# Last stage of an audio tower on one Trainium2 core: query/key/value at the end of the period in front, the norm ahead of them a period earlier, and another order of the experts' layers

## The reference, cut to what matters

```
h = tok(x)                                   # patches, matmul, norm: (32, 92, 128)
h = h + ssm(layernorm(h))                    # 16 states, a scan over time
h = h + moe(layernorm(h))                    # 6 experts, one chosen for each token
h = h + attn(layernorm(h))                   # window of 7 positions, 16 heads of 8
    q, k, v = x @ qkv_w.T + qkv_b
    p = softmax(q . k[window] * SCALE + rpb[...])      # 7 scores for each head
    attn = (sum over the 7 offsets of p * v[window]) @ proj_w.T + proj_b
h = h + ffn(layernorm(h))                    # 6 experts for each sequence
    ew = weights of 6 experts, from the mean over the sequence's tokens (router)
    ffn = sum over e of ew[e] * (gelu(x @ W1[e] + b1[e]) @ W2[e] + b2[e])   # 128 -> 341 -> 128
```

## Time and profile before

| | |
|---|---|
| median of 3 executions | 825.05 us (824.59 to 826.01) |
| the profiled execution | 826.72 us |
| its span, first to last instruction | 824.9 us |
| mean granted TensorE clock | 0.871 |
| busy: PE, PEld, DVE, ACT, POOL | 626.6, 475.1, 623.7, 518.4, 278.5 us |
| last stage, from about 542.6 us on | 282.3 us |

### The profile page before, as it was taken

One profiled execution on the slowest core, in us unless ns is written; L12 is line 12 of the kernel. 1 busy time (PEld: TensorE's weight loads), 2 busy tenths in 40 slices (PEclk: granted clock), 3 DMA queues, 4 the chain that ended last, 5 costly groups with the idle time before them and its releaser, 6 DMA issues.

```text
span 824.9 us, 10874 instructions
## 1 busy us (share of the span) xinstructions
PE 626.6 (76%) x3090; PEld 475.1 (58%) x3091; DVE 623.7 (76%) x1289; ACT 518.4 (63%) x821; POOL 278.5 (34%) x312
## 2 busy tenths in 40 slices
PE   6996751835637183659788799987899999999998
PEld 4563651835627173555565689844566666666665
DVE  1787598999999999999886122167698898896853
ACT  1587899899899998993243034352466466465452
POOL 0464000000000100000388244316357667664642
PEclk9997876958678695869767799999899999999999
DMA  5381042355444455540611366320000000000000
GB/s 181 112 292 49 1 86 41 73 99 107 73 86 86 73 102 98 92 86 0 224 33 39 102 175 191 90 65 1 1 0 7 4 11 8 2 10 7 5 10 18
DMA packets 26383, 56.50 MB, mean 68 GB/s; under 512 B 4203, under 2 KB 15572, under 8 KB 25860
## 3 DMA queue, kind: packets, MB, share of 16 engines
q0 software_dynamic: 5728, 24.56, 15.8%
q1 hardware_dynamic: 19848, 30.80, 12.2%
q10 hardware_dynamic: 764, 0.62, 0.2%
HBM read 29.91 MB, written 10.17 MB: 49 GB/s over the span
## 4 chain that ended last, share of the span: by engine, by line
PE 37%; DVE 27%; issue 15%; ACT 10%; POOL 5%; DMA 2%; POOLq 1%; SPq 1%; ACTq 0%; DVEq 0%
PE psum L2101 6%; PE psum L1797 4%; DVE s_R L1286 4%; DVE s_R L1273 4%; PE psum L2088 3%; POOL x_sorted L688 3%; PE psum L2016 3%; PE psum L2024 3%; DVE s_R L1297 3%; PE psum L1883 2%; PE psum L1884 2%; PE psum L1885 2%; PE psum L2090 2%; PE psum L2089 2%; PE psum L2191 2%
## 5 line engine op out<-in xcount | busy, mean ns | idle before, releaser
L1883 PE MATMUL psum<-s_xn_lo,s_split_hi 128*128 128x368 f32 x256 | 95.3, 372 | 134.9 <-ACT s_R L914 132.6
L1883 PEld LDWEIGHTS psum<-s_xn_lo,s_split_hi 128*128 128x128 f32 x256 | 55.0, 215 | 139.2 <-ACT s_R L914 135.3
L673 POOL DMA_DIRECT2D s_xnfm<-s_R x14 | 17.1, 1219 | 258.7 <-DVE s_R L1297 258.7
L1292 DVE TENSOR_TENSOR_SCAN s_R<-s_R 128x2944 f32<-128x2944 f32 x15 | 94.4, 6292 | 0.7
L1054 ACT ACTIVATE s_R<-psum,s_cols 128x368 f32<-128x368 f32 x96 | 50.3, 566 | 68.2 <-PE psum L2090 68.1
L1884 PE MATMUL psum<-s_xn_hi,s_split_lo 128*128 128x368 f32 x256 | 92.3, 361 | 0.0
L1885 PE MATMUL psum<-s_xn_hi,s_split_hi 128*128 128x368 f32 x256 | 91.9, 359 | 0.0
L2101 PE MATMUL psum<-s_R 128*128 128x368 f32 x256 | 90.5, 484 | 0.0
L732 POOL TENSOR_TENSOR s_R<-s_R 128x368 f32<-128x368 f32 x47 | 54.0, 1148 | 38.5 <-DVE s_R L1586 19.2
L769 POOL TENSOR_TENSOR s_R<-s_R 128x368 f32<-128x368 f32 x48 | 46.6, 970 | 57.7 <-DVE s_R L1722 56.9
L921 ACT ACTIVATE s_R<-psum,s_cols 128x736 f32<-128x736 f32 x64 | 56.1, 876 | 14.5 <-PE psum L1885 10.8
(11 more groups left out here) (260 smaller groups left out, 1617.0 us busy)
## 6 DMA issues: line engine op xcount, KB each, us to landing
s_xnfm<-s_R POOLq DMA_DIRECT2D x14, 1472.0 KB, 10.5
s_R<-in_w SPq DMA_DIRECT2D x28, 256.0 KB, 2.9
s_R<-in_xg SPq DMA_DIRECT2D x7, 744.0 KB, 4.2
x_sorted<-in_x_init SPq DMA_DIRECT2D x1, 5082.0 KB
s_wBC<-in_wBC SPq DMA_DIRECT2D x8, 256.0 KB, 2.6
s_R<-in_v SPq DMA_DIRECT2D x2, 1024.0 KB
s_R<-x_sorted SPq DMA_DIRECT2D x28, 66.0 KB, 2.4
s_R<-in_w SPq DMA_DIRECT2D x1, 1536.0 KB, 6.4
```

What stands on the lines that cost most here:

```text
L1292: dve.tensor_tensor_scan(bufB[:, u], ra[:, u], bufB[:, u], 0.0, ALU.mult, ALU.add).then_inc(ra_free, 1)
L1883: pe.matmul(bank(c), w_hi[:, s, u, k, :], xn_lo[:, a:b], start=True, stop=False)
```

## The change

Only the last stage is touched.

- PE: `qkv_of(c + 1)` stands at the end of period c, ahead of the last two tiles, `qkv_of(0)` ahead of the loop. The transposes of `norm_transposes(nE, c + 1)` stand in the middle of period c, ahead of `shares_fm`; their input is made a period earlier. `project` comes first in the period, then one tile, `scores`, one tile, `scores_tm`, and 8 tiles in a row. `fill_pause` is gone. `spread_out` names its two offsets.
- The list `FFN`: the rests' first layer comes as tiles 6 to 9, their second layer as 18 to 21; experts 3 and 4 have their first layer as 14 to 17; expert 5 is last with both layers. A chunk's units (6 experts and the rests) have their places in `UNITS`, and what counts units goes by `unit(f, e)`.
- DVE: `residual_stats` is split into `residual` and `stream_stats`, `first_experts` into itself and `experts_stats`. A period begins with the statistics of `experts_stats(c + 1)` left over from the one before, the experts' weights and `weigh_rest`, then the products; `scores_out` comes between `residual` and `stream_stats`. The 7 experts' units are weighed at other places. `first_experts(c + 2)` stands between offsets 1 and 2.
- ACT: `qkv_out(c + 1)` stands at the end of the period, `normed_e(c + 1)` at the start of the next; four gelus stand behind `stream_hi`, not ahead.
- POOL: `rstd_e(c + 2)` stands last in the period; `projection_bias`, `rstd_f` and the adds follow. `weighted_sum` is cut in four.

```diff
+        FFN = (pair(1, 0, 1, 2) + rest_of(1) + pair(2, 0, 1)
+               + pair(1, 3, 4) + rest_of(2) + pair(2, 2, 3, 4) + pair(1, 5) + pair(2, 5))
+        UNITS = (0, 1, NE, 2, 3, 4, 5)
...
             for c in range(NCH + 2):            # POOL
-                add_expert(c - 3, NE)
+                att = c < NCH
                 if 1 <= c <= NCH:
                     projection_bias(c - 1)
-                if c + 1 < NCH:
-                    rstd_e(c + 1)
-                add_expert(c - 2, 1)
+                    rstd_f(c - 1)
+                add_unit(c - 2, 1)
...
+                    weighted_sum(c, 3, 4)
+                if c <= NCH:
+                    add_unit(c - 2, 6)
+                if att:
+                    weighted_sum(c, 5, 6)
+                if c + 2 < NCH:
+                    rstd_e(c + 2)
...
+                if 1 <= c < NCH - 1:            # ACT
+                    normed_e(c + 1)
                 gelus(c - 2, 14, 16)
-                gelus(c - 2, 16, 18)
                 if c < NCH:
                     exponential(c)
-                gelus(c - 2, 22, 24)
+                    load_table(ACT.Gelu, 1)
+                rest_out(c - 2)
...
                     stream_hi(c - 1)
+                gelus(c - 2, 16, 18)
+                gelus(c - 2, 28, 30)
+                gelus(c - 1, 0, 10)
...
                     expert_weights(f - 1)       # DVE
-                weigh_expert(f - 1, 0)
-                weigh_expert(f - 1, 1)
...
+                weigh_rest(f - 1)
                 if att:
                     score_products(c)
...
-                store_chunk(c - 3)
                 if tail:
-                    residual_stats(f)
+                    residual(f)
                 if att:
                     scores_out(c)
+                if tail:
+                    stream_stats(f)
+                weigh_expert(f - 1, 0)
...
                 if att:                         # PE
                     scores(c)
-                ffn(f - 1, 18, 20)
+                ffn(f - 1, 15, 16)
                 if att:
                     scores_tm(c)
-                ffn(f - 1, 20, 22)
+                ffn(f - 1, 16, 24)
...
-                    if c >= 2:
-                        fill_pause(1)
                     shares_fm(c)
...
+                    spread_out(c, 0, 1)
...
+                ffn(f - 1, 26, 30)
+                ffn(f, 0, 1)
+                if tail:
+                    router_logits(f)
+                ffn(f, 1, 2)
+                if att:
+                    spread_out(c, 2, 3)
...
+                ffn(f, 6, 12)
+                if tail:
+                    router_spread(f)
                 if c + 1 < NCH:
-                    pe.wait_ge(pb_free, c * K + K - 1)
-                    norm_transposes(pe, nE, c % 2, c + 1, (7, 7))
+                    qkv_of(c + 1)
                 ffn(f, 12, 14)
```

More of the change, by code:

```diff
@@ L499, in audio_tower, with pair, rest_of @@
         out_done = [sem("out_done0"), sem("out_done1")]
-        FFN = ([(1, e, j) for e in (0, 1, 2) for j in range(FT)]
-               + [(2, e, j) for e in (0, 1) for j in range(FT)]
-               + [(1, 3, 0), (1, 3, 1)] + [(1, NE, r) for r in range(NR)]
-               + [(1, 4, 0), (1, 4, 1)] + [(2, e, j) for e in (2, 3) for j in range(FT)]
-               + [(1, 5, 0), (1, 5, 1)] + [(2, e, j) for e in (4, 5) for j in range(FT)]
-               + [(2, NE, r) for r in range(NR)])
+        def pair(layer, *es):
+            return [(layer, e, j) for e in es for j in range(FT)]
+        def rest_of(layer):
+            return [(layer, NE, r) for r in range(NR)]
+        FFN = (pair(1, 0, 1, 2) + rest_of(1) + pair(2, 0, 1)
+               + pair(1, 3, 4) + rest_of(2) + pair(2, 2, 3, 4) + pair(1, 5) + pair(2, 5))
+        UNITS = (0, 1, NE, 2, 3, 4, 5)
         ORDER1 = [(e, j) for layer, e, j in FFN if layer == 1]
@@ L762, in second_share, with weighted_sum @@
                 pool.tensor_tensor(zs[:, 1:2], euler, zs[:, 3:4], ALU.pow).then_inc(rt_exp, 1)
-            def weighted_sum(c, after_second):
-                for o in range(1, K):
+            def weighted_sum(c, *offsets):
+                for o in offsets:
                     pool.wait_ge(pb_free, c * K + o + 1)
@@ L1060, in rest_out @@
                     return
-                g = f * NU + NE
+                g = unit(f, NE)
                 act.wait_ge(fo_mm, g + 1)
@@ L1580, in weigh_expert @@
                     return
-                g = f * NU + e
+                g = unit(f, e)
                 if g >= 2:
@@ L1626, in score_products, with residual @@
                         .then_inc(prod_r, 1)
-            def residual_stats(c):
+            def residual(c):
                 dve.wait_ge(proj_mm, c + 1)
@@ L1730, in _ @@
                     expert_weights(f - 1)
-                weigh_expert(f - 1, 0)
-                weigh_expert(f - 1, 1)
-                if 0 <= f - 1 and not att:
-                    weigh_rest(f - 1)
-                if c + 1 < NCH:
-                    first_experts(c + 1)
+                weigh_rest(f - 1)
                 if att:
@@ L2172, in shares_fm, with spread_out @@
                 ins.then_inc(PT_ready, 1)
-            def spread_out(c, o):
-                if o % 2:
-                    return
+            def spread_out(c, o, *more):
+                two = (o,) + more
                 if o == 0:
@@ L2180, in spread_out @@
                     pe.wait_ge(P_fm_ready, c + 1)
+                    if 1 <= c < NCH - 1:
+                        pe.wait_ge(nE.xT_free, 2 + c + 2)
                     if c:
@@ L2185, in spread_out @@
                 else:
-                    pe.wait_ge(pb_free, c * K + min(o + 1, K - 1) - 2)
-                two = range(o, min(o + 2, K))
+                    pe.wait_ge(pb_free, c * K + two[-1] - 2)
                 for P, last in ((P_lo, False), (P_hi, True)):
@@ L2267, in _ @@
-                    norm_transposes(pe, nE, c % 2, c + 1, (7, 7))
+                    qkv_of(c + 1)
                 ffn(f, 12, 14)
-                if tail and not att:
-                    router_spread(f)
             result_last()
```

197 lines of the change are left out of this document (96 added, 101 removed).

## The result

| | before | changed |
|---|---|---|
| median of the runs, us | 825.14 (824.59 to 826.01, 4 runs) | 835.61 (835.31 to 836.22, 4 runs) |
| ratio changed / before | | 1.0119, 95% interval 1.0096 to 1.0143 |
| the profiled execution: time, span, us | 826.72, 824.9 | 836.22, 834.4 |

Forecast were 824.6 us, with a chance of 0.43 for slower, 0.41 for faster.

The account below looks back on a forecast made before the run. PE nearly binds, but DVE's chain through PE and POOL may decide. Middle periods -1.3, periods 0 and 1 -0.5, period 7 +0.4, tail +1.0: -0.4 us from 825.05, 824.6; range 816 to 836, likeliest case 820.5 to 829.

Parts of the forecast that it names:

- Rival (b): Middle periods: POOL stays shut out until the products end, residual at 10.1, period 32.75 us, total 834.9; chance 0.30.
- I am wrong if DVE has no idle time before the residual and yet the period is over 31: Middle period: the prediction's own condition for being wrong; the alternative condition was period 1's clock deciding the difference.
- case (a): Middle periods: POOL gets in between products, its bias holds DVE about 1.1 us, residual at 8.05, period 30.7; chance 0.45.
- an idle residual: Sign in the changed profile: residual with idle time ended by POOL, under 1 us for case (a), over 2 for (b).
- first_experts(1) ... +1.8: Period 0: this operation now stands ahead of the offsets, delaying the next query/key/value by 1.8 us; periods 0 and 1 together -0.5.
- The tail, +1.0: End of the kernel: second layers of experts 4 and 5 wait for gelus, last unit weighed on DVE; +1.0 us.
- Period 7, +0.4: Last period: the bias against `weigh_rest` again, +0.4 us.
- the middle period, 30.7: Five middle periods: 30.7 us each in case (a), against 30.96 before, -1.3 us in all.
- they wait some 0.15 for PE's router matmul: Start of DVE's middle period: the experts' weights wait some 0.15 us for the router matmul, which stands behind tile 11.
- this move: Middle period: `scores_out` comes earlier by the statistics' 1.2 us, which still precede the softmax, so only waits are saved.
- case (c): Middle periods: the bias costs nothing, period 29.9 us, total 820.3; part of the gain rival, chance 0.25.
- done in time: Middle period, offset 2 to the end: PE's work is ready when DVE needs it, so the stretch takes 7.1 us.

Follow-up runs that it names:

- e3: Changed kernel with POOL adding the projection's bias one period earlier, ahead of the first weighted sum; 832.01 us.
- e9: Changed kernel with one more unused power of 92x4 values on POOL ahead of the projection's bias, so it asks later; 841.15 us.
- e10: Changed kernel, period 0 alone: chunk 1's expert rows and statistics ahead of the score products, chunk 2's rows between shares and split; 830.85 us.
- e2: Changed kernel with filler matmuls nobody reads in PE's pauses of periods 0 and 1; 834.02 us.
- e6: Changed kernel with PE's tile order behind the last period rewritten, and some gelus and expert weighings moved there; 833.03 us.
- e5: Changed kernel with PE's spread of the router's result two second-layer tiles earlier; 833.10 us.
- e12: Changed kernel with ACT taking expert 4's two gelus ahead of the stream's copy; 834.16 us.
- e4: Changed kernel with PE's spreads of offsets 2 and 3 ahead of the next chunk's first tiles and router matmul, from period 1 on; 830.56 us.
- e11: e8 without its added fillers, one in period 0 and five in period 1; 814.81 us.
- e8: e7 plus the edits of e6 and e10, keeping one filler of three in period 0; 815.25 us.
- e7: Changed kernel with the edits of e2, e3, e4, e5 and e12 together; 821.94 us.

## Why the prediction was wrong

**What held.** That POOL and DVE meet at the bias and that it is let in between the products, at a cost of about 1.1 us (1.09 by e3, and wherever it asks, by e9). Rival (b), POOL shut out, is refuted as a mechanism, though its time (834.9) is close to the result, by chance: no row shows a residual that waits for POOL. The stretch from offset 2 to the end was 7.1, as said. And that offset 2 would wait for PE behind the gelus of expert 4. "I am wrong if DVE has no idle time before the residual and yet the period is over 31": that is what came, with 31.8. The other sign for case (a), an idle residual, was badly chosen: the bias is through before the products are, so the held product alone shows it.

**What failed, first: the ends.** They were given three short estimates, and the largest miss is there, 6.0 of 9.9 us.
- *"first_experts(1) ... +1.8"*, the two periods together -0.5: they were +2.0. The step left out is the second such operation, chunk 2's rows between offsets 1 and 2, and that the two together open the pauses after which the clock falls in period 0. e10 gives all 3.5 us back, e2 tells 2.5 of order from 1.0 of clock. The clock was named as open at 1 to 3 us; its price over periods 0 to 2 is 3.3 us by e2. Nor do the two terms given, +1.8 and -1.34, sum to -0.5: they make +0.5.
- *The tail, +1.0*: it was +3.5. Right were the two waits named (expert 4's gelus, 0.92 us; expert 5's, 0.76). Missing was that the new order runs the first layer in rows of four and of eight tiles with no attention work beside them: with two banks, nearly every pair waits 0.2 to 0.3 us for a gelu, and PE's waits behind 791.1 sum to 3.6 us. e6 takes 3.4 of 3.5 back.
- *Period 7, +0.4*: +1.4 by the cuts on PE. The prediction took the pair of tiles that PE owes less (1.34 us) off in period 1 and gave it back nowhere; period 7 has that pair more. Between the ends of the last offsets the period is 0.4 us longer than before, as said.

**Second: the middle period, 30.7, was 31.8.** The landmarks, us from the last offset:

| | predicted | measured |
|---|---|---|
| residual | 8.05 | 8.6 |
| end of the shares | 15.9 | 16.7 |
| offset 2 | 23.6 | 24.7 |
| end | 30.7 | 31.8 |

0.5 us came in ahead of the residual: "they wait some 0.15 for PE's router matmul", and it was 0.66. PE reaches L2220 behind tile 11 later than the layout had it. 0.2 us is `scores_out`, which waits 0.30 for PE's scores behind the residual. It does so in e3 too, where no product is held, so the waits that this move was to save stay with it in any case. 0.4 us is the way from the shares to offset 2 (8.1, not 7.7; the terms written out sum to 7.5). These three are readings of the landmarks; e5 and e12, which move the router's matmul and the gelus, gave back 0.23 and 0.44 of them. And e3, the period without the held product, is 30.69, where case (c) had 29.9. With case (a) the forecast's own sum of the five periods was -1.3; it was +2.7. That error of 4.0 us is what the text had allowed for ("some 4 us in all"), and it alone would have tipped the sign.

**Third: the layout followed DVE and took PE "done in time".** e4 and e5 show two of PE's steps in the chain's way, the spreads and the router's matmul, and that neither alone gives its whole gain back: a start 0.75 us earlier gave 0.23, 1.4 us less of wait gave 0.55. Behind the spreads the router's matmul stands next (e4); behind the router's matmul POOL's last sum and ACT's copy of the query do (e5). The change had not only a price, it had a gain that its own order of tiles hid: with four edits of order the middle period is 29.7, 1.3 us under before.

What stays open: ACT's copies and POOL's sums were not tried apart, so it is not known which of them keeps a freed wait from coming through. Why POOL's L738 was shut out for all seven products in before's rows and its operations are let in here, neither.

## What to carry to other kernels

When a change reorders a pipeline, lay out its first and last periods as carefully as the middle one: here they held 6.9 of the 9.5 us. In period 0 and at the end other chunks' work, which hides a step in the middle, is missing. A wait that one edit frees is worth only what the next one in line leaves. So lay out landmarks of the period, price moves together and not one by one, and ask of each engine when it arrives, not only of the one that seems to be the chain. What is taken off at one end of a pipeline has to be looked for at the other: the pair of tiles here was a loan. A regression made of several order mistakes can hide a change that pays: mend them one by one, each with a distance that it must move, before giving up the change.

## What the runs showed of the hardware

- The bias on POOL (92x512, 1.28 us alone), let in between two products of a DVE row, held the next one for 1.1 us, wherever in the row it came: the fourth product (1.60 in place of 0.51) or the seventh (1.59). The Trainium skill (SBUF — State Buffer, "Who interferes with whom") has the two exclude each other for a whole instruction; the bias agrees. The power of 92x4 values does not: L766 in e9 ran for 1.28 us while three products beside it took 0.51 each, so what it holds up of DVE, if anything, is far shorter than itself.
- The same pause of TensorE brought the clock down in one execution and not in another. e10 and e11 have the same PE work in period 0 (22.29 and 22.30 us) and the same pause at its end, 1.46 us up to 562.93 and 1.47 us up to 565.14. e10, then e11, windows of 2 us, columns as for e10 above:
```profile
560.00:562.00 2.00, 1.47 (x9) 1.00 0.00 0
562.00:564.00 2.00, 1.07 (x4) 1.00 0.00 0
564.00:566.00 2.00, 1.90 (x12) 1.00 0.00 0
```
```profile
562.00:564.00 2.00, 1.67 (x10) 1.00 0.00 0
564.00:566.00 2.00, 0.86 (x2) 0.70 0.00 0
566.00:568.00 2.00, 2.00 (x5) 0.50 0.00 0
```
Whether the clock fell in a single profile is therefore weak evidence for an edit. e2 and e8, with fillers in the pauses, had no fall in their profiles; e7, with all those of e2, had one.
- Half the clock cost little here, and about the same in two orders of the work. Over periods 0 to 2 the changed kernel spent 23.8 us at half clock and took 3.3 us more than e2, e11 spent 10.2 and took 1.4 more than e8: 0.14 us for each us. Each is a difference of two single profiles, with the fillers' own time in it.
